# A three-stage decoder layer on one core: hand-over work moved ahead of three stage boundaries

## The reference

```python
# x (2, 2048, 512), ctx_1024 (2, 154, 512)
x = x + linear_attention(layernorm(x))       # 16 heads of 32, 128 features, elu(.)+1; kv and k_sum over all 2048 keys
x = x + cross_attention(layernorm(x), ctx)   # 16 heads of 32, softmax over 154 keys
x = x + experts(layernorm(x))                # 8 experts (512 -> 256 -> 512), softmax router, 6 of 8 kept, shared FFN of 512
```

## Time and profile before

| | us |
|---|---|
| median of 3 runs | 2475.06 |
| the three runs | 2475.06, 2495.57, 2473.82 |
| the profiled execution | 2492.89 |
| its span, first to last instruction | 2491.1 |
| PE's first instruction of linear / cross / experts | 434.62 / 769.86 / 1244.67 |

### The profile page before, as it was taken

One profiled execution on the slowest core, in us unless ns is written; L12 is line 12 of the kernel. 1 busy time (PEld: TensorE's weight loads), 2 busy tenths in 40 slices (PEclk: granted clock), 3 DMA queues, 4 the chain that ended last, 5 costly groups with the idle time before them and its releaser, 6 DMA issues. The chain is left out here.

```text
span 2491.1 us, 33609 instructions
## 1 busy us (share of the span) xinstructions
PE 2378.9 (95%) x12584; PEld 1797.9 (72%) x12584; DVE 1351.6 (54%) x2168; ACT 1051.1 (42%) x1893; POOL 796.7 (32%) x755
## 2 busy tenths in 40 slices
PE   7999999999996999999789999999999999999998
PEld 6888886566665455555468887888888888888887
DVE  5555445777763355554554446544475444644444
ACT  3556565777741333343254444333243332433322
POOL 1444453424341032223477775111111111112111
PEclk9999995999996799999889999999999999999999
DMA  6655445666636344454255554644446444464442
GB/s 200 169 128 145 120 107 147 190 192 185 186 119 170 87 116 117 116 153 128 104 197 201 179 169 168 223 138 169 135 135 205 150 165 135 135 206 148 137 135 85
DMA packets 131857, 379.52 MB, mean 152 GB/s; under 512 B 14736, under 2 KB 40080, under 8 KB 113168
## 3 DMA queue, kind: packets, MB, share of 16 engines
q1 hardware_dynamic: 131440, 377.12, 49.2%
q10 hardware_dynamic: 256, 0.26, 0.0%
HBM read 246.20 MB, written 103.81 MB: 141 GB/s over the span
## 5 line engine op out<-in xcount | busy, mean ns | idle before, releaser
L2537 PE MATMUL ex_pg<-ex_xb,ex_wg 128*128 128x512 f32 x3360 | 822.8, 392 | 13.3 <-ACT ex_m L2204 6.8
L2537 PEld LDWEIGHTS ex_pg<-ex_xb,ex_wg 128*128 128x128 f32 x3360 | 632.8, 189 | 154.7 <-issue 12.4
L2553 PE MATMUL ex_pd<-ex_wd,ex_ht 128*128 128x512 f32 x1920 | 486.5, 389 | 2.9 <-issue 2.6
L2553 PEld LDWEIGHTS ex_pd<-ex_wd,ex_ht 128*128 128x128 f32 x1920 | 360.0, 188 | 79.1 <-issue 4.5
L2389 DVE SCALAR_TENSOR_TENSOR ex_acc<-ex_pd,ex_share,ex_acc 128x512 f32<-128x512 f32 x320 | 239.8, 749 | 302.4 <-PE ex_pd L2553 302.3
L2204 ACT COPY ex_m<-ex_pg 128x512 f32<-128x512 f32 x240 | 140.7, 586 | 385.0 <-PE ex_pg L2537 384.8
L2149 POOL TENSOR_TENSOR ex_h<-ex_g,ex_up 128x512 f32<-128x512 f32 x80 | 103.3, 1291 | 553.3 <-issue 469.0
L391 POOL TENSOR_TENSOR pr_ks_sum<-pr_ks_sum,pr_kp 128x512 f32<-128x512 f32 x128 | 165.0, 1289 | 176.9 <-DVE pr_kp L539 166.1
L2208 ACT ACTIVATE ex_g<-ex_g 128x512 f32<-128x512 f32 x160 | 101.2, 632 | 238.0 <-DVE ex_g L2365 165.6
L2141 POOL TENSOR_TENSOR ex_wd<-stage,ex_wd 128x512 fp32r<-128x512 f32 x80 | 105.5, 1342 | 260.1 <-ACT ex_wd L2185 260.1
L1466 ACT ACTIVATE cr_ring<-cr_s_bank 128x512 f32<-128x512 f32 x160 | 89.2, 602 | 163.1 <-PE cr_s_bank L1741 135.5
(11 more groups left out here) (212 smaller groups left out, 3478.1 us busy)
## 6 DMA issues: line engine op xcount, KB each, us to landing
ex_wg<-w_scratch SPq DMA_DIRECT2D x60, 1024.0 KB, 5.1
ex_wg<-w_scratch SPq DMA_DIRECT2D x60, 768.0 KB, 4.4
w_scratch<-ex_wg SPq DMA_DIRECT2D x20, 1792.0 KB, 6.8
stage<-in_units SPq DMA_DIRECT2D x60, 512.0 KB, 7.0
qk<-pr_kq SPq DMA_DIRECT2D x192, 128.0 KB, 2.4
qk<-q_scratch SPq DMA_DIRECT2D x96, 256.0 KB, 4.7
cr_q<-xq_scratch SPq DMA_DIRECT2D x96, 256.0 KB, 5.4
q_scratch<-pr_kq SPq DMA_DIRECT2D x128, 128.0 KB, 2.3
```

Of the source, the lines that this page charges most:

```text
L2537: mm = nc.tensor.matmul(pg[f][BANK[j]][:], wg[:, f, j, s, c * P:(c + 1) * P], xb[:, j, m, c * TB:(c + 1) * TB], start=(k == 0 and j in FRESH),
L2553: mm = nc.tensor.matmul(bank_of("D", n, i)[:], ht[:, s, f, k, t * P:(t + 1) * P], wd[:, n % 2, m, f * D:(f + 1) * D], start=(at == 0), sto ...
```

## The change

It has five parts. (1) In the last block of `project` the queries' pieces of group 0 are cut 6, 2, 2, 2 instead of 3, 3, 3, 3, and each stands ahead of its `kv`. (2) Work of the experts' start goes to the end of cross attention: the loads of `x_last` and of the router's weights (SP, behind the load of block 7's x), the weight sums (POOL, ahead of block 7's reciprocal), the high parts of the first weights (ACT, ahead of `turned`), their low parts (POOL, between block 7's reciprocals of the deviation), and two token sums (DVE, ahead of block 7's `divide`). For that the tiles are placed in both stages at the same addresses (`first`). POOL's order for block 7 has the low parts of the normalised result ahead of the bias. (3) The first context is loaded in the linear stage. (4) The first keys are placed by six DMAs of SP and six of ACT; POOL zeroes `k_w` by batch element, the second behind `context_values`. (5) The low part of `wo` is made behind the maxima of block 0, and PE waits for it at the first projection.

```diff
@@ project, PE, last block @@
+                    cuts = [MM // TT * t for t in range(TT + 1)] if g else [0, 6, 8, 10, MM]
                     for t in range(TT):
+                        if g == 0:
+                            piece((LAST, "Q", g), cuts[t], cuts[t + 1])
                         kv(LAST, TT * g + t)
                         if g + 1 < G:
                             features(LAST, TT * (g + 1) + t)
-                        piece((LAST, "Q", g), MM // TT * t, MM // TT * (t + 1))
                         if g:
+                            piece((LAST, "Q", g), cuts[t], cuts[t + 1])
                             head(HG * (g - 1) + t)
@@ attend_linear, SP @@
+                    if i == NBLK - 1 and s == 0:
+                        sp.wait_ge(h_full, H * (NBLK - 1))
+                        sp.dma_start(first.ctx[:], a["ctxT"][0].rearrange("(c p) n -> p c n", p=P))\
+                            .then_inc(first.sems["ctx_in"], 16)
@@ attend_cross, SP @@
-                load_context(0)
...
-                place_keys(0)
+                place_keys(0, range(HG // 2))
...
+                sp.wait_ge(s_full, SU * G * NBLK)
+                sp.dma_start(first.x_last[:], x3_part(x3_dram, X3_SLOTS)).then_inc(first.sems["x_in"], 16)
+                sp.dma_start(first.r_raw[:], a["router"].rearrange("(c p) n -> p c n", p=P))\
+                    .then_inc(first.sems["const_in"], 16)
                 stores(NBLK - 1)
@@ attend_cross, POOL @@
                 for b in range(NB):
+                    if b:
+                        pool.wait_ge(filled, POS[(0, "CV", 1)] + 1)
+                        pool.wait_ge(k_row, b)
                     nc.gpsimd.memset(k_w[:, b].bitcast(F32), 0.0).then_inc(k_zero, 1)
-                pool.wait_ge(k_zero, NB)
-                nc.gpsimd.memset(k_w[K3:ROWS, :, :, 0:KEYS].bitcast(F32), -1.0).then_inc(k_row, 1)
+                    pool.wait_ge(k_zero, b + 1)
+                    nc.gpsimd.memset(k_w[K3:ROWS, b, :, 0:KEYS].bitcast(F32), -1.0).then_inc(k_row, 1)
...
+                i = NBLK - 1
+                first_sums()
+                reciprocal_low(i, 0)
+                reciprocal_low(i, 1)
+                normalised_low(i)
+                add_bias(i, 0)
+                add_bias(i, 1)
+                reciprocal_std(i, 0)
+                add_bias(i, 2)
+                add_bias(i, 3)
+                reciprocal_std(i, 1)
+                first_low((0, 1))
+                reciprocal_std(i, 2)
+                first_low((2, 3))
+                reciprocal_std(i, 3)
+                first_low((4, 5, 6))
@@ attend_cross, ACT @@
                         context(0)
+                        act.wait_ge(dve_read, DVE_AT[(0, "CK", G - 1)])
+                        act.wait_ge(k_zero, 1)
+                        for r, s in enumerate((HI, HI, LO)):
+                            for j in range(HG // 2, HG):
+                                act.dma_start(key_rows(0, r, j), key_source(0, s, j)).then_inc(k_in, 16)
                         nc.scalar.copy(wo[:, HI], wo_raw).then_inc(w_hi, 1)
...
                 normalised(NBLK - 1)
+                act.wait_ge(num_full, G * NBLK)
+                act.wait_ge(next_in, 16 * (1 + FT + X3_SLOTS))
+                for j, source in enumerate(first_sources()):
+                    if j == 2:
+                        act.wait_ge(first.sems["sum_set"], 4)
+                    nc.scalar.copy(first.wg[:, 0, j, HI], source).then_inc(first.sems["w_hi"], 1)
                 turned(NBLK - 1)
@@ attend_cross, DVE @@
                         context_values(0)
+                        for g in range(G):
+                            maxima(mx(0, g))
                         dve.wait_ge(w_hi, 1)
                         nc.vector.tensor_tensor(wo[:, LO], wo_raw, wo[:, HI].bitcast(F32), ALU.subtract).then_inc(w_lo, 1)
-                        for g in range(G):
-                            maxima(mx(0, g))
...
+                b11, b12 = x3_slot(stage, 0), x3_slot(stage, 2)
+                dve.wait_ge(s_full, SU * G * NBLK)
+                dve.wait_ge(next_in, 16 * (1 + FT + X3_SLOTS))
+                nc.vector.tensor_tensor(first.t_a[:], b12, b11, ALU.subtract).then_inc(first.sems["t_set"], 1)
+                dve.wait_ge(first.sems["t_set"], 1)
+                dve.wait_ge(first.sems["x_in"], 16)
+                nc.vector.tensor_tensor(first.t_b[:], first.x_last[:], first.t_a[:], ALU.subtract)\
+                    .then_inc(first.sems["t_set"], 1)
                 divide(NBLK - 1)
@@ experts, POOL and ACT @@
-                weight_sums(0, 0)
-                weights_low(0, 0)
...
-                tokens_high(0, 0)
-                weight_high(0, 0, 0)
-                tokens_high(0, 1)
-                weight_high(0, 0, 1)
-                for j in range(2, MULS):
+                for j in range(MULS):
                     tokens_high(0, j)
-                    weight_high(0, 0, j)
@@ experts, DVE @@
-                token_sum(0, 0)
-                tokens_low(0, 0)
-                tokens_low(0, 1)
-                tokens_low(0, 2)
-                token_sum(0, 1)
-                tokens_low(0, 3)
+                for j in range(4):
+                    tokens_low(0, j)
```

More of the change, by code:

```diff
@@ L123, in decoder_kernel, with place @@
         x2_out, x3_out = whole.enter_context(nc.semaphore("x2_out")), whole.enter_context(nc.semaphore("x3_out"))
+        first = First()
+        with ExitStack() as places:
+            def place(name, shape, dt=F32):
+                return places.enter_context(nc.sbuf_tensor("first_" + name, shape, dt))
+            place("skipped", [P, 2 * FT * D * 2])
+            with nc.sbuf_tensor("first_keys", [P, H * (P + KPAD)], F32), nc.sbuf_tensor("first_ctx", [P, C, CTXW], F32) as ctx:
+                first.ctx = ctx
+            first.wg = place("wg", [P, FT, MULS, 2, 2 * P], F32R)
+            place("skipped2", [P, 4 * TB])
+            first.sums = place("sums", [P, 4, 2 * P])
+            first.r_raw = place("r_raw", [P, C, P])
+            first.x_last, first.t_a, first.t_b = [place(name, [P, 2 * TB]) for name in ("x_last", "t_a", "t_b")]
+        for name in ("ctx_in", "x_in", "const_in", "sum_set", "w_hi", "w_lo", "t_set"):
+            first.sems[name] = whole.enter_context(nc.semaphore("first_" + name))
         with ExitStack() as linear:
@@ L144, in decoder_kernel, with __init__, a_rows @@
             attend_linear(nc, a, NBLK, BLK, x_blk, q_dram, x1_dram, xq_dram, ident, f_w, qk3, q_in, q_out, xq_out, kv_w, ks_w, qp,
-                          first_heads, wq, half, stage)
-        attend_cross(nc, a, NB, BLK, x1_dram, xq_dram, x2_dram, x3_dram, xq_out, x2_out, x3_out, ident, half, stage)
-        experts(nc, a, NB, BLK, x2_dram, x3_dram, w_dram, x2_out, x3_out, out_bat, ident, stage)
+                          first_heads, wq, half, stage, first)
+        attend_cross(nc, a, NB, BLK, x1_dram, xq_dram, x2_dram, x3_dram, xq_out, x2_out, x3_out, ident, half, stage, first)
+        experts(nc, a, NB, BLK, x2_dram, x3_dram, w_dram, x2_out, x3_out, out_bat, ident, stage, first)
+class First:
+    def __init__(self):
+        self.sems = {}
+def a_rows(stage, f, row, half):
+    at = (2 * row + half) * 2 * P
+    return unit_slot(stage, f)[:, at:at + 2 * P]
 def load_group(sp, q_dram, b, g, q3, landed):
@@ L728, in attend_linear @@
 def attend_linear(nc, a, NBLK, BLK, x_blk, q_dram, x1_dram, xq_dram, ident, f_w, q3, q_in, q_out, xq_out, kv_w, ks_w, qp,
-                  first_heads, wq, half, stage):
+                  first_heads, wq, half, stage, first):
     SLOTS, PER, HBANKS, BANKS = 8, 2, 3, 3
@@ L1206, in unit_slot, with attend_cross @@
     return stage[:, part * X3_PART:(part + 1) * X3_PART]
-def attend_cross(nc, a, NB, BLK, x1_dram, xq_dram, x2_dram, x3_dram, xq_out, x2_out, x3_out, ident, half, stage):
+def attend_cross(nc, a, NB, BLK, x1_dram, xq_dram, x2_dram, x3_dram, xq_out, x2_out, x3_out, ident, half, stage, first):
     SU = HG + 1
@@ L1321, in attend_cross, with key_rows, key_source, context_of @@
         K_DMAS = 3 * HG
+        def key_rows(b, r, j):
+            return k_w[r * HD:(r + 1) * HD, b].rearrange("p (g j) k -> p g j k", j=HG)[:, :, j, 0:KEYS].bitcast(F32)
+        def key_source(b, s, j):
+            return k_nat[b][j * HD:(j + 1) * HD, s, :, 0:KEYS].bitcast(F32)
+        def context_of(b):
+            return ctx_t if b else first.ctx
         def bank_of(*key):
@@ L1327, in slot_of, with first_sources @@
             return (G * i + g) % QRING
+        def first_sources():
+            return [a_rows(stage, 0, 0, 0), a_rows(stage, 0, 0, 1)] + [first.sums[:, k] for k in range(4)] + \
+                [a_rows(stage, 0, 1, 1)]
         with nc.Block() as block:
@@ L1824, in out_proj @@
                         g, (s, m) = n // 3, PASSES[n % 3]
+                        if i == 0 and t == 0 and n == 0:
+                            pe.wait_ge(w_lo, 1)
                         if t == 0 and n % 3 == 0:
```

(18 more changed lines are left out.)

90 lines of the change are left out of this document (53 added, 37 removed).

## The result

| | before | after |
|---|---|---|
| median of 20 executions each | 2476.2 us | 2469.98 us |
| lowest and highest | 2470.33, 2496.22 | 2463.88, 2475.01 |
| profiled execution, its span, mean clock | 2492.89, 2491.1, 0.967 | 2473.69, 2471.9, 0.976 |

The estimated ratio of after to before is 0.9954, 95% interval 0.9937 to 0.9972, within the 1% that was called no change; the two medians of the table alone give 0.9975. The forecast was 2472.6. Five of the 20 executions of before lie between 2489 and 2497, none of after does; without these five the median of before is 2475.57, so the change is worth 5.6 us against the shorter kind and removes the longer one.

What follows compares the result with a forecast made beforehand. PE was taken to run at full clock except at three places where stages meet, each bound by its own wait. From the profiled 2492.89: -17.8 - 6.0 + 3.5 = 2472.6 us; range 2460 to 2491.

Steps and rivals of the forecast that it cites:

- end of `project`, against the longer kind: Queries ahead of `kv` keep PE's clock full, so the 41.0 us stretch takes 23 to 25: -17.8 us against the profile.
- the same, against the median: End of `project`: nothing gained against the median, as the shorter kind of run was taken to have full clock there already.
- start of cross attention: From the stage's start to block 0's maxima: context there early, keys placed sooner, `wo` moved; -6.0 us (ends -4 and -8).
- divide behind `x_last`: End of cross attention: second token sum waits for `x_last`, `divide` is queued behind it; reciprocal 9.4 us late (5.7 to 12).
- POOL's low parts first: End of cross attention: POOL makes the result's low parts ahead of the bias, which held it 2.50 us; -2.1 us.
- experts' start: Two sums leave the chain before PE's fourth product (-3.2), POOL's weight sums come earlier (-1.1): -4.3 us (ends -2 and -7).
- part 2 in all: End of cross attention and experts' start together: 9.4 - 2.1 + 0.5 - 4.3 = +3.5 us (ends -4 and +9).
- the clock falls anyway: Rival, end of `project`: PE stays at half clock despite the new order; 2490.4 us, chance 0.17.
- PE then works on without a gap: End of `project`: six queries fill PE's 0.87 us wait, first `kv` starts about 1 us later, no idle time follows.
- Six by each are out after 4.5 us, 3.2 earlier: Start of cross attention: twelve key copies split over SP and ACT issue in 4.5 us instead of 7.70, bringing keys 3.2 earlier.
- Now the values are late next: Start of cross attention: with keys at 779.1, DVE finishes the values and goes to the maxima at 780.3 to 782.4.
- the 16 that were named as a sign: Start of cross attention: maxima beginning some 16 us after the stage's first DMA issue instead of 23.

## Why the prediction was right, step by step

| step | predicted | measured |
|---|---|---|
| end of `project`, against the longer kind | -17.8 | -18.6 in its stretch |
| the same, against the median | 0 | 0 (2475.10 for 2474.8, the shorter kind beside it) |
| start of cross attention | -6.0 | -3.8 in the profile, -5.9 by runs |
| divide behind `x_last` | +9.4 | +10.3 |
| POOL's low parts first | -2.1 | -2.0 |
| barrier | +0.5 | +0.2 |
| experts' start | -4.3 | -7.4 |
| part 2 in all | +3.5 | +1.2 in the profile, +0.75 by runs |

The forecast lies 2.6 us over the median; the term of part 2 is the one that was too high by about as much.

**Part 1** was right in mechanism and size, and right that the median doesn't show it. Only "PE then works on without a gap" did not come: 0.93 us of idle time stand at 399.29 us, without harm. The reasoning from the gap of 17.8 us between profile and median found the one stretch that could hold it. The rival "the clock falls anyway" leaned on a rule of the Trainium skill (TensorE: Matmul & The Clock Gate, Why this matters for your kernels), a section that warns only of idle gaps several times as long. The two kernels with three queries in front disagree with it: an idle time of 0.99 us in one, none worth a row in the other, and the half clock in six of twelve executions against none.

**Start of cross attention**: the sum was right, two of its steps were not. The step "Six by each are out after 4.5 us, 3.2 earlier" failed as a gain: issue did get shorter (3.86 us of SP), landing rose from 2.2 to 5.0 (8.4 for the slowest), and the run with one queue has the same time. While SP alone issued the copies, the DMA engines were at a share of 0.46 for 7.7 us, so by my estimate the copies need about 3.5 us of all of them, and behind the query loads these weren't free. The step "Now the values are late next" failed too: DVE was through with them 15.4 us after the entry, a little sooner than the 15.7 to 17.8 forecast, but the keys came at 16.8 to 17.6 in eight of nine profiles, not at 14.5. So the maxima began 17.4 us after the entry or later, not at the 16 that were named as a sign. That the two errors cancel in the sum is luck. What stands is the context's wait: it was 6.9 to 8.1 us in the five profiles without the early context and 2.5 in the nine with it, 4.8 less in the mean, and the rest of the way to the score is 38.0 to 40.2 us in seven of the nine profiles with the early context (41.3 in two), against 39.7 to 40.6 in the five others.

**Part 2**: the wait was sized well. The load took 9.5 us where the profile's own row for x gave 7.7 plus a little. The rule of the Trainium skill (DMA: Bandwidth & Descriptors, Anatomy of one DMA), which is stated there for DMAs that GpSimd issues and not SP, gave 3.2 us; the run with `x_last` ahead of x has 3.8, close to it. So here it comes near a load that finds the engines free, and `x_last` in the change did not. The mis-sized term is the experts' start. Of its 4.3 us, 3.2 were for the fourth product, which came 4.4 sooner, and 1.1 for what lies behind it, where it was 3.0: ACT no longer waited 1.47 us for POOL's sums in front of its first activation, PE's second stop of 1.39 us went, and DVE's wait for PE's next product, in the middle of the router work, fell from 2.82 to 0.35. From the entry to this group it is 26.6 to 26.9 us in all seven profiles with part 2 and 34.0 in six of the seven without; in the last one it is 31.6, with the twelve matmuls behind PE's second stop taking 3.01 us instead of 5.41, so a part of this term hangs on the clock. These rows stood in the trace of before, and following the chain to the point from which PE ran without waits would have found them.

**No change within 1%** followed: the gain is 5 to 6 us of the 24.8 that make one per cent, and none of it comes from part 2, the part with the most code.

## What to carry to other kernels

When a profile and the median disagree by more than the usual scatter, look for the stretch at half clock that fits the difference, and fill the idle time ahead of it: that changes how often an execution is long, not the median. Work moved ahead of a critical operation on the same engine must have its data there already; here the place of one load in SP's order was worth 10 us. Before splitting DMA issues over two queues, take the share of the DMA engines while one queue issues, multiply by its time, and ask what else those engines must move then.

## What the hardware showed that I had not expected

The two programs whose profiles show an idle time of 0.87 or 0.99 us on PE at this place had 47 executions of the longer kind in 143 (131 of them with 0.87 us, 12 with 0.99); those without it had none in 120. Both profiles of the longer kind have some 40 us at half clock behind it. At 0.93 to 0.95 us of idle time some 20 us later the clock held in all twelve profiles with full clock before it, and behind the 0.77 us in block 7's scores it fell in one and held in the other.

DVE's subtraction of two operands of 128x1024 in SBUF took 1.75 us while POOL was adding (1184.80, POOL's sums from 1183.86 to 1187.8) and 1.22 us while POOL was idle (1197.59). With `x_last` earlier, the second of these two sums ran beside POOL too and took 1.64. The Trainium skill (GPSIMD Engine Reference, 1. Specifications) says that POOL's way into SBUF is shared with DVE, and that DVE instructions with two SBUF inputs contend for it; these rows agree. The delay can fall on POOL instead: with the second sum later, DVE's took 1.23 us and the POOL instruction beside it 2.30, where the three others of its row took 1.27.
